# A third PSUM bank for first-layer attention scores, and one bank for the early jobs

## The reference: two gated cross-attention layers, a quantised and a routed feed-forward

```python
x = x + tanh(g_xattn[0]) * attention0(layernorm(x), ctx, mask0)   # 16 heads of depth 8
x = x + tanh(g_ffn[0])   * quantised_ffn0(layernorm(x))           # Hadamard, 4-bit rows, ternary weights
x = x + tanh(g_xattn[1]) * attention1(layernorm(x), ctx, mask1)   # 16 heads of depth 64
x = x + tanh(g_ffn[1])   * routed_ffn1(layernorm(x))              # 32 experts, best 4 per token, one shared

def attention(q_in, ctx, mask):
    q, k, v = q_in @ Wq.T + bq, ctx @ Wk.T + bk, ctx @ Wv.T + bv   # split into heads
    scores = where(mask, q @ k.T / sqrt(depth), very_negative)
    return softmax(scores) @ v @ Wo.T + bo
```

## Time and profile before

| what | before |
|---|---|
| median of three runs | 275.84 us (275.27 to 276.56) |
| span of the profiled execution, first to last instruction | 273.6 us |
| the profiled execution's own time | not given apart from its span |
| instructions | 6702 |
| busy: TensorE / its weight loads | 252.8 us (92%) / 200.2 us (73%) |
| busy: VectorE / ScalarE / GpSimd | 212.9 us (78%) / 191.3 us (70%) / 181.2 us (66%) |
| granted TensorE clock, mean | 0.999 |

### The profile page before, as it was taken

How to read it: one execution, slowest core, us unless ns; L and a number is a source line. 1 busy time by engine, 2 the same in 40 slices (tenths; PEclk the granted TensorE clock), 3 DMA queues, 4 the chain that set the end, 5 groups by cost and what they waited for, 6 DMA issues and landing times.

```text
span 273.6 us, 6702 instructions
## 1 busy us (share of the span) xinstructions
PE 252.8 (92%) x1903; PEld 200.2 (73%) x1903; DVE 212.9 (78%) x654; ACT 191.3 (70%) x454; POOL 181.2 (66%) x271
## 2 busy tenths in 40 slices
PE   7987998999788999999999999999989999979994
PEld 5555666666556777777777888777777778878993
DVE  3799898889978896979778777777798625985673
ACT  2578798889697886965777666677776664656462
POOL 7357999777679776646664475449757795936380
PEclk9999999999999999999999999999999999999999
DMA  6557565300005666534475667756542051211530
GB/s 194 193 169 219 223 229 134 103 2 4 1 9 115 146 140 135 129 84 106 99 216 149 175 173 186 190 126 174 129 127 60 11 149 38 85 34 39 185 112 19
DMA packets 25987, 32.91 MB, mean 120 GB/s; under 512 B 4000, under 2 KB 18144, under 8 KB 25824
## 3 DMA queue, kind: packets, MB, share of 16 engines
q1 hardware_dynamic: 25520, 32.27, 43.8%
q10 hardware_dynamic: 432, 0.22, 0.3%
HBM read 14.32 MB, written 3.47 MB: 65 GB/s over the span
## 4 chain that ended last, share of the span: by engine, by line
PE 67%; DVE 11%; issue 9%; POOL 9%; ACT 3%; DVEq 0%; POOLq 0%; ACTq 0%
PE bank L1229 16%; PE bank L1398 14%; PE bank L1360 5%; PE bank L1234 5%; PE bank L1236 5%; PE bank L1235 5%; PE bank L1361 5%; PE bank L1354 4%; POOL q L648 3%; DVE masked L943 2%; POOL probs L604 2%; PE bank L1421 2%; PE bank L1413 2%; PE bank L1478 1%; DVE probsT L960 1%
## 5 line engine op out<-in xcount | busy, mean ns | idle before, releaser
L604 POOL TENSOR_SCALAR probs<-probs,rsum 128x512 f32<-128x512 f32 x128 | 87.9, 693 | 57.4 <-DVE rsum L952 56.5
L747 ACT ACTIVATE probs<-masked,neg_max 128x512 f32<-128x512 f32 x128 | 91.9, 719 | 11.9 <-DVE neg_max L943 9.1
L1229 PE MATMUL bank<-ident,probs 128*128 128x128 f32 x512 | 77.9, 275 | 0.8 <-ACT probsT L756 0.8
L1229 PEld LDWEIGHTS bank<-ident,probs 128*128 128x128 f32 x512 | 60.0, 141 | 14.6 <-issue 8.2
L943 DVE CUSTOM_DVE_ANT_0 masked<-bank,mask 128x512 f32<-128x512 f32 x64 | 43.8, 684 | 15.3 <-PE bank L1361 14.8
L756 ACT ACTIVATE probsT<-bank 128x512 f32<-128x512 f32 x74 | 43.5, 588 | 16.2 <-PE bank L1229 15.9
L1398 PE MATMUL bank<-probsT,val 128*32 128x256 f32 (+1 forms) x512 | 46.6, 384 | 0.0
L960 DVE COPY probsT<-bank 128x512 f32<-128x512 f32 x54 | 36.7, 680 | 11.4 <-PE bank L1229 11.1
L943 DVE CUSTOM_DVE_ANT_0 masked<-bank,shared 128x512 f32<-128x512 f32 x64 | 43.3, 677 | 0.4 <-PE bank L1354 0.3
L1354 PE MATMUL bank<-parts 128*128 128x512 f32 x64 | 31.3, 490 | 8.9 <-DVE neg_max L943 8.7
L1398 PEld LDWEIGHTS bank<-probsT,val 128*32 128x32 f32 (+1 forms) x512 | 24.4, 123 | 17.7 <-issue 5.1
(11 more groups left out here) (238 smaller groups left out, 525.4 us busy)
## 6 DMA issues: line engine op xcount, KB each, us to landing
k_both<-k_low SPq DMA_DIRECT2D x32, 128.0 KB, 2.8
k_both<-k_high SPq DMA_DIRECT2D x32, 128.0 KB, 2.7
q<-q_split SPq DMA_DIRECT2D x32, 128.0 KB, 2.4
probsT<-staged_gate SPq DMA_DIRECT2D x32, 128.0 KB, 3.0
q<-q_split SPq DMA_DIRECT2D x32, 64.0 KB, 2.1
parts<-staged_k SPq DMA_DIRECT2D x7, 256.0 KB, 2.8
w_flat<-in_w SPq DMA_DIRECT2D x1, 1536.0 KB, 8.0
staged_k<-k_high SPq DMA_DIRECT2D x2, 512.0 KB, 3.1
```

The lines of the kernel that those rows point to most:

```text
L604: pool.tensor_scalar(p, p, rsum[:, u % NCOL:u % NCOL + 1], 1.0, ALU.mult, ALU.mult).then_inc(normed, 1)
L747: act.activation(probs[:, u % NP, :], masked[:, u % NS, :], ACT.Exp, scale=-1.0, bias=neg_max[:, c:c + 1], accum_out=sums[:, c:c + 1]).the ...
L1229: ins = pe.transpose(dst[0:rows, t * P:t * P + P], src, ident[:, :])
```

## The change

Three things are changed.

- The scores of the first layer rotate through three banks, 0, 1 and 6. Unit u waits for the maximum of unit u - 3 there. In the second layer they still alternate between banks 0 and 1, with the parity turned round, so that unit 64 follows unit 61 in bank 1 and unit 65 follows unit 63 in bank 0.
- All jobs of steps before 60 use bank 5 alone; from step 60 on they alternate between 5 and 6 as before. The first job that goes to bank 6 again, the first of the second layer's values at step 60, waits for the maximum of the last unit that used the bank. The five jobs ahead of the loop are spread over four banks: k0 in 5, kn in 6, the first layer norm's turn in 7, q0 in 3, and qn in 5 again.
- Some jobs move in the plan: k9 from step 55 to 54, q9 from 57 to 56; for the second batch of the first layer qn from 14 to 15 and v0 from 15 to 17; `turn_fw` from 18 to 21. k8, q8, k10 and all later ones stay.

```diff
+JOB_BANKS = 4
+TWO_BANKS_AT = 60
...
-        plan.setdefault(k.first - early - (13 if k.g or k.b else 15), []).append(("k", k.m))
-        plan.setdefault(k.first - early - (11 if k.g or k.b else 12), []).append(("q", k.m))
+        plan.setdefault(k.first - early - (14 if k.m == 9 else 13 if k.g or k.b else 15), []).append(("k", k.m))
+        plan.setdefault(k.first - early - (12 if k.m < 10 else 11), []).append(("q", k.m))
     for n, name in enumerate(("kn", "qn", "v0")):
-        plan.setdefault(LN01_AT + 7 + n, []).append((name, 1))
+        plan.setdefault(LN01_AT + 7 + 2 * n, []).append((name, 1))
...
-    plan.setdefault(18, []).append(("turn_fw",))
+    plan.setdefault(21, []).append(("turn_fw",))
...
-    place, count = {}, [0, 0, 0]
+    one_bank = [j for t in plan if t < TWO_BANKS_AT for j in plan[t]]
+    place, count = {}, [0] * JOB_BANKS
     for j in order:
-        i = 2 if j == ("logits", 1) else 1 if j in last else number[j] % 2
+        if j in before or j == ("logits", 1):
+            i = {"k": 0, "kn": 1, "ln": 2, "logits": 2, "q": 3, "qn": 0}[j[0]]
+        else:
+            i = 1 if j in last else 0 if j in one_bank else number[j] % 2
...
+SECOND_BANK = next(j for j in PLACE if PLACE[j] == (1, 1))
...
+def score_home(u):
+    return u % 3 if u < L1_AT else (u + 1) % 2
+
+def maxed_before(u):
+    return max((v + 1 for v in range(u) if score_home(v) == score_home(u)), default=0)
...
-        score_bank = bank[0:2]
+        score_bank = [bank[0], bank[1], bank[6]]
...
-        job_banks = bank[5:8]
+        job_banks = [bank[5], bank[6], bank[7], bank[3]]
...
+                if j == SECOND_BANK:
+                    pe.wait_ge(maxed, L1_AT - 1)
...
-                dst = score_bank[u % 2][:, :]
+                dst = score_bank[score_home(u)][:, :]
...
-                if u >= 2:
-                    pe.wait_ge(maxed, u - 1)
+                if maxed_before(u):
+                    pe.wait_ge(maxed, maxed_before(u))
+                elif score_home(u) == 2:
+                    pe.wait_ge(*freed(("kn", 0)))
```

More of the change, by code:

```diff
@@ L392, in build @@
         job_done = sem("job_done")
-        job_free = [sem("job_free0"), sem("job_free1"), sem("logits_free")]
+        job_free = [sem("job_free0"), sem("job_free1"), sem("logits_free"), sem("first_q_free")]
         half_done = sem("half_done")
@@ L942, in mask_max @@
                 c = u % NCOL
-                dve.tensor_tensor_reduce(out=masked[:, u % NS, :], in0=score_bank[u % 2][:, :], in1=mask,
+                dve.tensor_tensor_reduce(out=masked[:, u % NS, :], in0=score_bank[score_home(u)][:, :], in1=mask,
                                          scale=-float(k.depth) ** -0.5, scalar=3.0e38, op0=ALU.add, op1=ALU.min,
```

## The result

The changed kernel takes **272.47 us** (median of four runs, 272.21 to 273.05) against 275.55 for the kernel before in the same comparison (274.55 to 276.56): a ratio of 0.9897, with a 95% interval of 0.9873 to 0.9922. By that ratio it is 2.84 us less (an interval of 0.8 to 1.3%), and 3.08 by the two medians, where 3.07 were forecast. The profiled run took 272.69 us with a span of 270.7, at a granted TensorE clock of 0.997.

What follows compares the result with a forecast made beforehand. First-layer time was put down to VectorE's waits behind mixes, with TensorE the bound in the second layer. 1.4 + 0.9 + 0.97 - 0.2 = 3.07 us less, 275.84 to 272.8; range 270.6 to 276.3.

Steps and rivals of the forecast that it cites:

- the 14.3 us of TensorE: First-layer score weight loads waiting for the maximum; taken as mostly slack of an engine ahead, and not counted.
- (a): Rival: GpSimd is no bar and all five stalls behind mixes return, 5.18 us, giving 270.7; chance 0.07.
- (b): Rival: no gain, as turn banks hold turns and mixes where they were; 275.7; chance 0.20 together with (d).
- (c): Rival: slower, as k9, q9 and k10 pay whole evictions on the single job bank; +2.6, 278.4; chance 0.12.
- (d): Rival: a job still sits in bank 6 and holds its scores; 275.8; chance 0.20 together with (b).
- The first three mixes: First-layer mixes with 3.18 us of VectorE stalls; 1.4 us returned together, limited by GpSimd's queue.
- So a single mix loses all of its stall: Step: with the score 0.97 us earlier, VectorE's wait of about 1 us behind a lone mix vanishes.
- the fourth mix: Mix at 57.64 us, free of GpSimd's lateness after its 1.46 wait; 0.9 of its 1.03 stall returned.
- inside the 1.4 above, which GpSimd sets: v0's possible wait for qn's low part, 0.48 us, just before the second mix; claimed to cost nothing extra.
- the sixth: Mix at 79.70 us: it goes 1.4 us earlier and VectorE's stall of 0.97 goes entirely.
- The border: Between the layers: k9, q9 and k10 wait for readouts in the single job bank; 0.2 us lost.
- The moves: Jobs shifted in the plan: k9 and q9 one step earlier cost nothing; later qn and v0 stay within 1.4 us.

Runs made afterwards that it cites:

- e1: The changed kernel, but each first-layer score waits for the maximum of the unit two before, as with two banks: 275.59 us, ratio 1.0004.
- e5: The changed kernel with a fourth turn bank (bank 5) for units 22 to 34: 271.81 us, ratio 0.9872.
- e9: The changed kernel with a fourth score bank (bank 5) for units 28 to 39: 271.93 us, ratio 0.9885.
- e2: The changed kernel with GpSimd's four conversions of the second mask moved from steps 12 to 18 to steps 36 to 42: 273.47 us, ratio 0.9916.
- e4: The changed kernel with all moved jobs put back to their old steps: 274.07 us, ratio 0.9952.
- e7: The changed kernel with the second batch's v0 moved to step 20, behind the second mix, and its values two steps later: 273.32 us, ratio 0.9924.
- e6: The changed kernel with GpSimd normalising only 256 of 512 columns of each first-layer unit: 272.59 us, ratio 0.9895.
- e11: The changed kernel with the single job bank kept up to step 72 instead of 59: 277.54 us, ratio 1.0088.
- e10: The changed kernel with the first layer's three turn banks taken in an order shifted by one: 271.82 us, ratio 0.9877.

## Why the prediction was right, and where by luck

**Right:** the place (the waits behind the mixes, not the 14.3 us of TensorE), the sign, the size, and that the saving reaches the end unaltered. Rivals (a) and (b) fall with the waits shown first, (c) with the time, and (d) with e1.

**The first three mixes: 1.4 predicted, 1.40 measured (0.67 + 0.06 + 0.67), in good part by luck.** The step that failed is "So a single mix loses all of its stall". At the fourth mix, kernel after, maxima, the copy that frees a turn bank, and weight loads of the turn, the score and the mix:

```profile
53.58 0.67 DVE L979 COPY probsT<-bank 128x512 f32<-128x512 f32 x1
54.17 0.68 DVE L962 CUSTOM_DVE_ANT_0 masked<-bank,shared 128x512 f32<-128x512 f32 x1
54.37 0.42 PEld L1248 LDWEIGHTS bank<-ident,probs 128*128 128x128 f32 x4 [0.54 <-POOL probs L623]
54.85 0.67 DVE L962 CUSTOM_DVE_ANT_0 masked<-bank,shared 128x512 f32<-128x512 f32 x1
54.92 0.19 PEld L1377 LDWEIGHTS bank<-parts 128*128 128x128 f32 x1
55.35 1.45 PEld L1421 LDWEIGHTS bank<-probsT,val 128*32 128x32 f32 x32 [0.24 <-issue]
```

and the same place before, from the maximum that released the score:

```profile
56.48 0.67 DVE L943 CUSTOM_DVE_ANT_0 masked<-bank,shared 128x512 f32<-128x512 f32 x1
...
57.21 0.19 PEld L1354 LDWEIGHTS bank<-parts 128*128 128x128 f32 x1
```

From the end of that maximum to the copy, TensorE's chain (score, mix, turn) takes 60.20 - 57.15 = 3.05 us before and 57.91 - 54.85 = 3.06 after. Meanwhile VectorE has a copy and two maxima before, 2.02 us, and three maxima and a copy after, 2.70. The rest is the wait: 1.03 and 0.36. One bank more puts one more maximum into the cover, **0.67 us**; I had taken the mean of a unit, 0.97, which has half a copy in it that does not lie there. The turn in front waited for its bank, which the copy of 53.58 frees at 54.25, though its row names GpSimd: with a bank of its own (e5) it waits for nothing, and then the score waits for its maximum. That another score bank takes the remaining 0.36 is not shown: e5 and e9 each removed one condition and found another right behind it. At the fourth mix both at once need two banks, where one is free; at the third, a fourth score bank together with e2's later masks needs none. Neither was tried.

**The second mix gave 0.06, not a third of 1.4.** Kn, qn and v0 share the bank, and v0 stands right in front of that mix: 0.43 of waiting and 0.97 of products (e4's second fence). I had seen the wait, and put it "inside the 1.4 above, which GpSimd sets"; it was the bar itself, with GpSimd next in line (e7).

**GpSimd** is dense as foreseen, one wait of 0.8 us between 25 and 52, and at the third mix it stands where the prediction put it: the mix was forecast for 47.34, 35.00 from the first maximum of the kernel before, and came at 35.01, by the chain of normalisation, turn and score that the prediction names (e9). But the bank, which the prediction took to be out of the way, allows the same moment: e2 and e6 relieve GpSimd alone and e9 the bank alone, and none of them shortens the wait by more than 0.03. That two gains of 0.67 and one of 0.06 met the queue's 1.4 is coincidence. At the second mix GpSimd is next in line, and at the first and the fourth the waits stay with GpSimd relieved. A queue without gaps is not late by that.

**The fourth mix** 0.66 (0.9 predicted), the same mis-sized 0.67; **the fifth** 0.06 (0); **the sixth** 1.06 (0.97), as argued; **the start** 0.23 within its scatter (0).

**The border** cost 0.38, where 0.2 were predicted for the job bank. q9 waits 0.73 for k9's readout (up to 0.75 predicted), k9 and k10 nothing. But the score of unit 64 waits 0.74 for q8's copies, which I had at nothing: "that costs nothing while SP waits for jobs". q8's four issues run from 82.33 to 85.73, one of them 1.42 long. In e11, where that one took 1.01, the copy of unit 58 comes 0.39 earlier, so the job bank itself cost about nothing there, and the whole 0.38 is the long issue.

**The moves** were costed at nothing and give nothing by themselves (e1), but they hold 1.5 of the gain (e4). The Trainium skill, Perfetto Trace Analysis, section Optimizing Tensor Performance (Matmuls), has independent matmul groups rotate through PSUM banks so that readouts overlap products. e1 shows no price for breaking that as long as the scores' wait for two banks sets the time; e11 shows 5.1 us (277.54 less 272.47) where jobs follow each other and TensorE is the bound. The trace agrees with the rule there, and in e4 and at the second mix too, where a job close behind its forerunner waited 0.43 to 1.21 us.

## What to carry to other kernels

Price one more buffer by the instruction that the consumer runs between two releases, not by the mean time of a round: take the producer's chain from the release to the waiting row, subtract what the consumer does meanwhile, and look at the next conditions within a few tenths before counting more. In these runs a shared buffer was free where its users stood further apart than a readout, so the order of the users belongs to the change, and should be tried with it. Where two resources rotate, try one rotation shifted against the border: e10's line gave 0.69 us in the trace, 0.65 by the medians.

## What had not been expected of the hardware

- The first maximum began anywhere from 11.23 to 12.66 us in 14 profiled runs with nearly one program: 1.4 us of scatter, half of the effect measured.
- Issues of like DMAs on SyncE's queue (the copies of the second layer's keys and queries) mostly take 0.46 to 0.67 us, and now and then one takes far longer: 1.42 at 83.00, right where TensorE waited for it. The same issue took 0.61 in the kernel before, e1 and e6, 0.74 in e7, and 1.01 to 1.48 in the other ten profiles. What sets its length was not tested.
- The same small VectorE instruction (the second batch's variance, 128x2, between 12 and 30 us) took 0.56 to 0.59 us in thirteen profiles and 0.17 in e6, where GpSimd ran half of its normalisation: 0.39 of the 0.58 us that e6 was ahead. What causes it was not tested.
